# The last expert stage of a two-layer transformer kernel: one block, scaled rows delivered by adding writes

## The reference

```python
x = hidden_states                      # layernorm of the residual, 1024 x 256
confidences = sigmoid(x @ conf_w.T + conf_b)
bids = confidences * wealth            # 8 experts
top_bids, selected_experts = top_k(bids, 2)
routing_weights = softmax(top_bids)
combine = sum(one_hot(selected_experts) * routing_weights)
expert(x) = (silu(x @ gate.T) * (x @ up.T)) @ down.T      # inner size 1024
output = sum over experts of expert(x) * combine
out = residual + output
```

## Time and profile before

| What | Value |
|---|---|
| Time, median of 3 runs | 1272.21 us (1271.94 to 1273.88) |
| The profiled execution: its time, its span | 1274.95 us, 1273.2 us |
| PE busy over the span | 1144.7 us, 90% |
| DVE, ACT, POOL busy | 559.2 us (44%), 447.6 us (35%), 207.4 us (16%) |
| DMA | 169.43 MB, mean 133 GB/s |

### The profile page before, as it was taken

One profiled execution on the slowest core, in us unless ns is written; L12 is line 12 of the kernel. 1 busy time (PEld: TensorE's weight loads), 2 busy tenths in 40 slices (PEclk: granted clock), 3 DMA queues, 4 the chain that ended last, 5 costly groups with the idle time before them and its releaser, 6 DMA issues. The chain is left out here.

```text
span 1273.2 us, 19035 instructions
## 1 busy us (share of the span) xinstructions
PE 1144.7 (90%) x7144; PEld 726.4 (57%) x7168; DVE 559.2 (44%) x1586; ACT 447.6 (35%) x586; POOL 207.4 (16%) x336
## 2 busy tenths in 40 slices
PE   7989999999769999999577999999984599999993
PEld 4443333333558888888443333333244599999993
DVE  4757777771561111111365776666325212112222
ACT  4646666667321111111032455555642011111010
POOL 4652222224000000000113000000200111111110
PEclk8989999999869999999877999999995799999997
DMA  8656222002152444453149022210003799998843
GB/s 218 166 154 150 38 38 39 1 1 99 67 199 50 155 176 167 164 179 68 54 181 191 13 44 41 41 21 1 1 1 134 275 359 316 324 320 315 310 144 108
DMA packets 85956, 169.43 MB, mean 133 GB/s; under 512 B 7825, under 2 KB 58721, under 8 KB 83314
## 3 DMA queue, kind: packets, MB, share of 16 engines
q1 hardware_dynamic: 80050, 157.85, 39.8%
q0 software_dynamic: 2208, 6.03, 1.6%
q10 hardware_dynamic: 3616, 4.46, 1.2%
HBM read 148.34 MB, written 19.79 MB: 132 GB/s over the span
## 5 line engine op out<-in xcount | busy, mean ns | idle before, releaser
L1191 ACT ACTIVATE prob<-st_ps 128x1024 f32<-128x1024 f32 x256 | 253.9, 1022 | 188.7 <-PE st_ps L1089 105.5
L217 DVE CUSTOM_DVE_ANT_0 junk<-s_ps,bias_rows,mx 128x512 f32<-128x512 f32 x236 | 168.0, 748 | 64.1 <-PE s_ps L202 63.3
L1081 PE MATMUL st_ps<-q_stack,k_stack 100*128 100x512 bf16 x512 | 186.0, 387 | 10.4 <-ACTq L1170 3.5
L202 PE MATMUL s_ps<-k_stack,q_stack 97*128 97x512 bf16 x468 | 178.4, 391 | 11.0 <-DMA q_stack<-q_scr 6.3
L217 DVE CUSTOM_DVE_ANT_0 junk<-s_ps,bias_rows 128x512 f32<-128x512 f32 x232 | 153.3, 689 | 78.9 <-PE s_ps L202 78.3
L1577 PE MATMUL h_ps<-expert_in,w 128*128 (+1 forms) x704 | 155.0, 382 | 2.2 <-PEq L65 2.2
L1577 PEld LDWEIGHTS h_ps<-expert_in,w 128*128 128x128 f32 (+1 forms) x704 | 132.8, 189 | 22.9 <-issue 2.4
L1101 PE MATMUL o_ps<-prob,v_unit 128*32 128x512 f32 x1024 | 140.1, 601 | 1.0 <-ACT prob L1191 1.0
L202 PEld LDWEIGHTS s_ps<-k_stack,q_stack 97*128 97x128 bf16 x468 | 45.5, 99 | 146.0 <-DVE mx L217 82.4
L1980 ACT ACTIVATE silu<-gu_ps 128x512 f32<-128x512 f32 x46 | 27.5, 597 | 225.9 <-PE gu_ps L1936 225.9
L1607 ACT ACTIVATE gelu_out<-h_ps 128x256 f32<-128x256 f32 (+1 forms) x88 | 33.7, 383 | 182.2 <-PE h_ps L1577 182.2
(11 more groups left out here) (277 smaller groups left out, 1146.9 us busy)
## 6 DMA issues: line engine op xcount, KB each, us to landing
wg<-in_gateT SPq DMA_DIRECT2D x23, 1024.0 KB, 5.7
wu<-in_upT SPq DMA_DIRECT2D x23, 1024.0 KB, 9.2
wd<-in_downT SPq DMA_DIRECT2D x23, 1024.0 KB, 11.6
w<-in_w SPq DMA_DIRECT2D x16, 1368.0 KB
w<-in_w SPq DMA_DIRECT2D x8, 1280.0 KB
k_scr<-k_parts SPq DMA_DIRECT2D x48, 128.0 KB, 2.3
k_stack<-k_scr SPq DMA_DIRECT2D x16, 384.0 KB, 5.2
k_stack<-k_scr SPq DMA_DIRECT2D x16, 256.0 KB, 5.7
```

What stands on the lines that cost most here:

```text
L202: pe.matmul(self.ps[:, self.bank("job", u, j)], stack(self.pr.Q[b], MROW, i % 2, h, slice(qt * P, (qt + 1) * P)), stack(self.pr.K[b], MROW ...
L217: self.pr.nc.vector.tensor_tensor_reduce(out=self.junk[:, self.bank("job", u, j)], in0=self.ps[:, self.bank("job", u, j)], in1=self.m.bias ...
L1081: pe.matmul(st_ps[:, h], stack(K[b], ROWS, i % 2, h, slice(kt * P, (kt + 1) * P)), stack(Q[b], ROWS, i % 2, h, slice(0, SQ)), start=True, ...
L1191: nc.scalar.activation(prob[:, kt % 2, 2 * hp:2 * hp + 2], st_ps[:, 2 * hp:2 * hp + 2], ACT.Exp).then_inc(exp_done, 1)
```

## The change

The two blocks become one, with no barrier and no clearing of semaphores between router and tiles. In it:

- PE runs 14 transposes into the unused `xt_ps` before the norm's transposes and 20 after the 16 products (`stay_warm`).
- The rank comes from PE alone: `chosen` is bf16 with a ninth, empty group, and one product by the triangular matrix plus eight by ones accumulate all running sums (9 bf16 matmuls in place of 2 fp32 ones). The running sum over experts is a product with a comparison table `sooner` (made by POOL) and a reduction. The tile number comes from two scalings with rounding in place of 22 comparisons and a reduction.
- Of the 16 `hot_row` tables DVE makes 13 in one operation, POOL the last 3, one each; of the `hot_token` tables DVE makes the first column set, ACT the other two.
- `rows` is written before anything else that follows the products; `share`, `dest` and a new list `place` come after it.
- SP writes `pr.x` to the first 1024 rows of `row_scr`, and 128 more rows for the dump, right after the weights of tile 0. It then waits for `share`, writes it to DRAM (`shares`), and loads the weights of tile 1: gate at once, up and down only when `xg` of tiles 0 and 1 has landed.
- Per tile, POOL fetches one routing weight per row by a third indirect DMA (`fetch_share`), DVE multiplies the result by it as it copies it out of PSUM, and the delivery adds to `row_scr` (`compute_op=ALU.add`). Rows that stand for nothing go to the 128 dump rows.
- The output is two DRAM to DRAM transfers of 512 KB from `row_scr`; the reading back, the 16 DVE operations and the 8 writes are gone.

The removed side of the router stands in the code printed above. The core of the diff:

```diff
+        tps, lps, rps, ips = gu_ps[:, 0:2], gu_ps[:, 2], gu_ps[:, 3], y_ps[:, 0]
...
+        OWN = 13
...
+                load_gate(sp, 0, 0)
+                load_others(sp, 0, 0)
+                sp.dma_start(t["row_scr"][0:TOK].rearrange("(t p) d -> p t d", p=P), pr.x[:]).then_inc(x_saved, 16)
+                sp.dma_start(t["row_scr"][TOK:TOK + P], pr.x[:, 0]).then_inc(x_saved, 16)
+                sp.wait_ge(share_done, 1)
+                sp.dma_start(shares.rearrange("(t p k) -> p t k", p=P, k=2), share[:]).then_inc(share_out, 16)
+                sp.wait_ge(table_done, 1)
...
-                    load_weights(sp, e, T % NS)
+                    load_gate(sp, e, T % NS)
+                    if T == 1:
+                        for s in range(2):
+                            sp.wait_ge(xg_in[s], 16)
+                    load_others(sp, e, T % NS)
...
                 all_sent(sp)
-                for half in range(2):
...
-                for g in range(NT):
-                    sp.wait_ge(x_done, NT + g + 1)
-                    sp.dma_start(t["out"][g * P:(g + 1) * P], pr.x[:, g]).then_inc(x_out, 16)
...
+                for n in range(2):
+                    at = slice(n * TOK // 2, (n + 1) * TOK // 2)
+                    sp.dma_start(t["out"][at], t["row_scr"][at]).then_inc(x_out, 16)
...
+                g.tensor_scalar(sooner[:], below[:], 0.0, None, ALU.is_gt).then_inc(fill_done, 1)
+                pool.wait_ge(spot_done, 1)
+                pool.wait_ge(iota_done, 5)
+                for n in range(OWN - NT, NT):
+                    g.tensor_scalar(hot_row[:, NT + n], line[:], spot[:, 1, n:n + 1], None,
+                                    ALU.is_equal).then_inc(row_done, 1)
+                pool.wait_ge(rows_done, 1)
+                pool.wait_ge(y_out, 16)
...
+                def fetch_share(T):
+                    if T == 0:
+                        pool.wait_ge(dest_done, 1)
+                        pool.wait_ge(share_out, 16)
+                    if T >= 2:
+                        pool.wait_ge(y_copied, T - 1)
+                    pool.indirect_dma_start(out=row_share[:, T % 2], out_offset=None, in_=shares.unsqueeze(1),
+                                            in_offset=bass.IndirectOffsetOnAxis(ap=place[:, T:T + 1], axis=0),
+                                            bounds_check=2 * TOK - 1).then_inc(rs_in[T % 2], 16)
...
+                    if T == 0:
+                        pool.wait_ge(x_saved, 32)
...
-                    pool.indirect_dma_start(out=t["row_scr"],
+                    pool.indirect_dma_start(out=t["row_scr"][0:TOK + P],
                                             out_offset=bass.IndirectOffsetOnAxis(ap=dest[:, T:T + 1], axis=0),
-                                            in_=y_row[:, T % 2], in_offset=None,
-                                            bounds_check=3 * TOK - 1).then_inc(y_sent[T % 2], 16)
+                                            in_=y_row[:, T % 2], in_offset=None, bounds_check=TOK + P - 1,
+                                            compute_op=ALU.add).then_inc(y_sent[T % 2], 16)
...
+                fetch_share(0)
+                fetch_share(1)
...
+                    if T + 2 < TILES:
+                        fetch_share(T + 2)
...
+                def stay_warm(n):
+
+                    for _ in range(n):
+                        pe.transpose(xt_ps[:, 0, 0:P], pr.ident[:], pr.ident[:])
+
+                stay_warm(14)
...
+                pe.wait_ge(fill_done, 4)
+                pe.wait_ge(c_done, 1)
+                flat = chosen[:].rearrange("p g e -> p (g e)")
+                pe.matmul(rps[:, 0:(NT + 1) * E1], lower_bf[:], flat, start=True, stop=False)
+                for far in range(1, NT + 1):
+                    mm = pe.matmul(rps[:, far * E1:(NT + 1) * E1], ones_bf[:], flat[:, 0:(NT + 1 - far) * E1],
+                                   start=False, stop=(far == NT))
+                mm.then_inc(r_ready, 1)
+
+                pe.wait_ge(tok_done, 4)
+                for n in range(2 * NT):
+                    if n == 0:
+                        pe.wait_ge(own_row, 1)
+                    elif n >= OWN:
+                        pe.wait_ge(row_done, n - OWN + 1)
+                    mm = pe.matmul(ips[:, 0:3 * TILES], hot_row[:, n],
+                                   hot_token[:, n].rearrange("p o t -> p (o t)"),
+                                   start=(n == 0), stop=(n == 2 * NT - 1))
+                mm.then_inc(i_ready, 1)
+                stay_warm(20)
...
+                act.dma_start(t["y_scr"].rearrange("(t p) d -> p t d", p=P), pr.y[:]).then_inc(y_out, 16)
...
+                act.wait_ge(step_done, 1)
+                act.wait_ge(iota_done, 5)
+                nc.scalar.activation(hot_token[:, :, 1], hot_step[:], ACT.Copy, scale=low_t[:, 0:1]).then_inc(tok_done, 1)
+                for k in range(2):
+                    mine = slice(k * NT, (k + 1) * NT)
+                    nc.scalar.activation(hot_token[:, mine, 2], hot_step[:, mine], ACT.Copy,
+                                         scale=float(k + 1)).then_inc(tok_done, 1)
+                act.wait_ge(diff_done, 1)
+                nc.scalar.activation(low[:], low[:], ACT.Exp).then_inc(exp_done, 1)
...
+                v.tensor_tensor(chosen[:, 0:NT], one[:, 0], one[:, 1], ALU.add).then_inc(c_done, 1)
+                v.tensor_tensor(low[:], top[1][:], top[0][:], ALU.subtract).then_inc(diff_done, 1)
...
+                dve.wait_ge(r_ready, 1)
+                dve.wait_ge(iota_done, 5)
+                count = rps[:, NT * E1:(NT + 1) * E1]
+                link(v.tensor_tensor(fills[:], count.unsqueeze(2).broadcast_to([P, E1, TOK // P]),
+                                     part_line[:].unsqueeze(1).broadcast_to([P, E1, TOK // P]), ALU.is_gt))
+                link(v.tensor_reduce(parts[:], fills[:], AX.X, ALU.add))
+                link(v.tensor_scalar(parts[:], parts[:], 1.0, None, ALU.max))
+                link(v.tensor_tensor(below[:], sooner[:], parts[:].unsqueeze(1).broadcast_to([P, E1, E1]), ALU.mult))
+                link(v.tensor_reduce(start[:], below[:], AX.X, ALU.add))
+                link(v.scalar_tensor_tensor(out=rank[:], in0=by_e(start[:]), scalar=float(P),
+                                            in1=rps[:, 0:NT * E1].rearrange("p (g e) -> p g e", g=NT),
+                                            op0=ALU.mult, op1=ALU.add))
+                link(v.tensor_tensor(pick[:], one[:], rank[:].unsqueeze(1).broadcast_to([P, 2, NT, E1]), ALU.mult))
+                link(v.tensor_reduce(slot_f[:], pick[:], AX.X, ALU.add))
...
+                link(v.tensor_scalar(full[:], slot_f[:], 1.0 / P, 0.5 / P - 0.5, ALU.mult, ALU.add))
+                link(v.tensor_scalar(full[:], full[:], ROUND, ROUND, ALU.add, ALU.subtract))
+                v.scalar_tensor_tensor(out=spot[:], in0=full[:], scalar=-float(P), in1=slot_f[:],
+                                       op0=ALU.mult, op1=ALU.add).then_inc(spot_done, 1)
+                v.tensor_tensor(hot_step[:], full[:].rearrange("p k g -> p (k g)").unsqueeze(2)
+                                .broadcast_to([P, 2 * NT, TILES]),
+                                line[:, 0:TILES].unsqueeze(1).broadcast_to([P, 2 * NT, TILES]),
+                                ALU.is_equal).then_inc(step_done, 1)
+                dve.wait_ge(spot_done, 1)
+                v.tensor_tensor(hot_row[:, 0:OWN], spot[:].rearrange("p k g -> p (k g)")[:, 0:OWN].unsqueeze(2)
+                                .broadcast_to([P, OWN, P]), line[:].unsqueeze(1).broadcast_to([P, OWN, P]),
+                                ALU.is_equal).then_inc(own_row, 1)
+                dve.wait_ge(step_done, 1)
+                v.tensor_tensor(hot_token[:, :, 0].rearrange("p (k g) t -> p k g t", k=2),
+                                hot_step[:].rearrange("p (k g) t -> p k g t", k=2),
+                                high[:].unsqueeze(1).unsqueeze(3).broadcast_to([P, 2, NT, TILES]),
+                                ALU.mult).then_inc(tok_done, 1)
+                link(v.tensor_tensor(end[:], start[:], parts[:], ALU.add))
+                link(v.tensor_tensor(past[:], end[:, 0:7].unsqueeze(1).broadcast_to([P, TILES, 7]),
+                                     line[:, 0:TILES].unsqueeze(2).broadcast_to([P, TILES, 7]), ALU.is_le))
+                link(v.tensor_reduce(expert[:], past[:], AX.X, ALU.add))
+                v.tensor_copy(table[:], expert[:]).then_inc(table_done, 1)
+                dve.wait_ge(i_ready, 1)
+                rank_of = ips[:, 2 * TILES:3 * TILES]
+                link(v.tensor_copy(token_f[:, 0], ips[:, TILES:2 * TILES]))
+                v.scalar_tensor_tensor(out=rows[:], in0=ips[:, 0:TILES], scalar=float(P),
+                                       in1=token_f[:, 0], op0=ALU.mult, op1=ALU.add).then_inc(rows_done, 1)
+                dve.wait_ge(exp_done, 1)
+                link(v.tensor_scalar(top[0][:], low[:], 1.0, None, ALU.add))
```

(34 more changed lines are left out.)

286 lines of the change are left out of this document (87 added, 199 removed).

## The result

The changed kernel takes 1254.79 us in the median of 4 runs (1252.90 to 1255.87) against 1272.08 in the same comparison: a ratio of 0.9861, 95% interval 0.9845 to 0.9876. The forecast was 1250.9 with 1246 to 1259, so the measured time is 3.9 us above the forecast and inside the range. The profiled execution took 1254.66 us with a span of 1253.0; before, 1274.95 and 1273.2. So the profiles differ by 20.3 us, where the forecast had 21.3, and the medians by 17.3. Medians of the same kernel differ by up to 2.6 us from one comparison to the next (the kernel before: 1272.1 to 1274.7), so kernels of different comparisons are set beside each other by their ratios.

What follows compares the result with a forecast made beforehand. PE never waits between tiles, so only time ahead of tile 0 and behind tile 22 could be won. Gains of 21.3 us took the profiled 1274.95 to 1253.7, less 2.74 for the median: 1250.9 us, range 1246 to 1259.

Steps and rivals of the forecast that it cites:

- Norm and logits: Start of the last stage: 14 idle transposes raise PE's clock to 2.4 GHz; gain 3.4 us, bounds 0 and 4.6.
- Chain to the ranks: Router, from `chosen` to `fills`: nine bf16 products replace fp32 products, copy and running sums; gain 2.0 us.
- Tables and products: Router, from `spot_in` to the copy of the result: tables split over DVE, ACT and POOL; gain 0.9 us.
- Barrier: Between the copy of the result and the first indirect DMA: barrier gone, other work moved behind; gain 1.5 us.
- First gather: Ahead of tile 0: less weight traffic beside it, landing after 4.2 us instead of 6.47; gain 2.3 us.
- Clock of tile 0: Tile 0's first 64 matmuls: 20 idle transposes raise the clock, 9.11 us becomes 7.15; gain 1.9 us.
- Tile 1 and on: Tile 1's up and down weights wait for the second gather, about even; cost 0.3 us, bounds 0 and 3.
- End: Behind the last delivery's start: adding write, DRAM to DRAM copy and closing take 11.0 us instead of 19.5; gain 8.5.
- Rival 1: Norm and tile 0: the transposes don't hold the clock, both gains are lost; 1256.2 us, chance 0.13.
- Third transfer per tile: In each tile: POOL issues three indirect DMAs instead of two; cost 0 while an adding write lands within a tile.
- rival 4: Between tiles: adding writes set the pace once a landing exceeds 10.0 us; 1370 us, chance 0.04.
- Rival 2: At the end: adding write lands after 7.7 us and the copy takes 8.1; 1256.6 us, chance 0.12.

Runs made afterwards that it cites:

- e4: Changed kernel, but SP writes `share` and loads all three weights of tile 1 only once the first gather has landed: 1256.49 us, ratio 0.9868.
- e7: Changed kernel with `share` written to DRAM as 128 pieces of 64 bytes instead of 1024 of 8 bytes: 1254.79 us, ratio 0.9851.
- e11: e10, but SP loads all three weights of tile 1 without waiting for any gather: 1251.20 us, ratio 0.9815.
- e1: Changed kernel without both rows of idle transposes, the 14 and the 20: 1258.83 us, ratio 0.9882.
- e0: The changed kernel measured again, unaltered, as yardstick: 1254.48 us, ratio 0.9864.
- e8: e7, but SP loads up and down of tile 1 after the first gather alone, not the second: 1251.51 us, ratio 0.9828.
- e9: Changed kernel with the old end: plain deliveries, reading back, DVE, eight writes, no `share` or `pr.x` in DRAM: 1262.33 us, ratio 0.9916.
- e10: e8 with 30 idle transposes instead of 20 behind the 16 products: 1250.52 us, ratio 0.9810.
- e2: Changed kernel with 50 idle transposes instead of 20 behind the 16 products: 1254.76 us, ratio 0.9858.
- e6: Changed kernel with all 16 `hot_row` tables made on DVE, none on POOL: 1256.97 us, ratio 0.9874.

## Why the prediction was right, and where it was not

Term by term, in the two profiles, forecast and found (differences as in the section on the result):

| Term | Forecast | Found |
|---|---|---|
| Norm and logits | 3.4 | 4.25 |
| Chain to the ranks | 2.0 | 2.36 |
| Start of each expert | 0.5 | 0.49 |
| Tile number | 0.6 | 0.69 |
| Tables and products | 0.9 | 1.19 |
| Barrier | 1.5 | 1.38 |
| First gather | 2.3 | 0.85 |
| Clock of tile 0 | 1.9 | -0.41 |
| Tile 1 and on | -0.3 | -0.3 |
| End | 8.5 | 9.05 |
| Sum | 21.3 | 19.5 |

The stage began 0.65 us earlier in the profile after, which makes the 20.2 of the spans.

That the sum came out so near is partly luck: the gather and tile 0's clock fell short by 3.8 us together, the barrier by 0.1, and the other terms won 2.1 more than forecast.

- **Norm and logits**: right in mechanism, and the clock held for all of it, nearly the bound of 4.6. But not always: in e4, e7 and e11 `bids` came after 11.5 us, in the other eight profiles with the transposes after 9.5. The 14 are worth 2.3 or 4.3 by execution, and e1, without them, is at 13.8. The profiles show what went before. First the changed kernel, then e7, the 14 transposes and the first of the norm:

```profile
960.37 3.18 PE L1830 MATMUL xt_ps<-ident 128*128 128x128 f32 x14 [2.26 <-PEq L66]
963.74 1.30 PE L747 MATMUL gu_ps<-ident,y_tok 128*128 128x128 f32 x8 [0.19 <-DVE y_tok L731]
```

```profile
961.20 2.86 PE L1830 MATMUL xt_ps<-ident 128*128 128x128 f32 x14 [2.26 <-PEq L66]
964.58 1.30 PE L747 MATMUL gu_ps<-ident,y_tok 128*128 128x128 f32 x8 [0.52 <-DVE y_tok L731]
```

  The clock left over from attention fell later in the three: PEclk is 0.69 to 0.73 in the stage's first microsecond, 0.50 to 0.55 in the eight. So the 14 were done 0.3 us sooner and PE paused 0.5 us behind them instead of 0.2; the clock rose all the same and fell again some 7 us into the stage, with PE at work without a break. A few more transposes, to close that pause, are the obvious test; no run made it.
- **The DVE terms** were right within 0.4 us. Durations per column and per link carried over; where I was low, in the chain to the ranks, PE's nine products took 0.47 us instead of the 0.73 reckoned at 0.081 each, at the same granted clock of 0.50; they have 72 to 8 columns, the row's 69.
- **First gather**: the mechanism that I priced, less weight traffic beside it, is real, but the step "The write of `share` is 1024 pieces of 8 bytes, whose cost no row shows" was mis-sized. I put 0.5 us on it, and it was 1.9 to 2.4 (5.6 here and 6.1 in e0 against 3.7 in e7). Of the kernels with the new router, those that write it so right before the gather have gathers of 5.6 us or more; the others (e4, e7, e8, e9, e10, e11) are under 5.
- **Clock of tile 0**: wrong. The step that failed is "the gather lands 0.1 + 0.4 + 0.8 + 4.2 = 5.5 after that, so they do not delay it". I asked only whether the transposes would be too many. The last ones ran at 2.4 GHz, so the 20 took 3.7 us instead of 4.9, the gather came 1.4 us later, and the gap of 3.5 us lost what they had won: tile 0 took 9.4 us, not 7.15. Rival 1 was right for this half of the change and wrong for the other.
- **Tile 1's weights**: even, as forecast: the down weights landed at 1001.5, and tile 1's first gate matmul began at 1001.55. But that is luck. They were complete 12.8 us after the first gather and not 10, and PE wanted them just as much later, because tile 0 was slow. With tile 0 as fast as forecast PE waits, as e2 shows with 1.7 us: the two errors hid each other, and the slack of zero is why e2's gain turned into a wait.
- **Third transfer per tile, adding writes**: nothing between the tiles (241.7 us with them in e1, e6 and e11, as before), and landings rose only to 8.7 at most against 7.7, under the 10.0 at which rival 4 begins. One of my reasons against it was misread, though: not only the first third of the tiles has a full DMA load. In the profile before the DMA share is 0.85 to 1.05 in every stretch from 1010 to 1226.
- **The end**: forecast 11.0 from the last delivery's start, found 10.3; the add 0.4 and the copy 0.3 less than taken. The other figure for the copy, 4.4, was 1.3 too low by the same reckoning (6.6 us from its first issue to the end, less 0.9 for the closing). Rival 2 falls.
- **From the profile to the median**: the step "It ran 2.74 above the median of 1272.21, which I take off at the end" does not hold up. 31 more executions of the kernel before lie between 1270.7 and 1276.5 with medians of 1272.9 to 1274.7, so 1274.95 was no outlier, and a median of three may be off by as much as the step. Without it the forecast is 1253.7, against 1254.79; but that compares one execution's base with a median. The medians of the same comparison differ by 17.3 and 18.5 us (e0), the stages by 19.5 and 18.6. So of the 3.9 us by which the forecast was low, 1.8 are the stage's, and the rest no part of the stage accounts for.

What stays open: why the stages before it end up to 8 us apart in different profiles, e6's gather of 7.2 us, and whether more transposes ahead of the norm would hold the clock in every execution.

## What to carry to other kernels

Idle matmuls before a stage pay when they end where its work begins: measure the pause behind them, and remember that they run twice as fast once the clock is up. A wait that lets the clock fall costs more than its length: 2.5 us became 4.4 in e7, and 5.7 became 8.0 in e4. Before a small table goes to DRAM, count its pieces and not its bytes: an 8 KB write delayed a gather on the critical path by 2 us and, where it stood ahead of weights in their queue, held those up for about 4 (e4). And where a change frees time ahead of a prefetch with no slack, move the prefetch in the same change, or the gain becomes its wait.

## What the hardware showed that I had not expected

- A DRAM write of 1024 pieces of 8 bytes landed after 4.5 us; behind one, the transfer engines moved only 29 to 57 GB/s for 4 us (e4). As 128 pieces of 64 bytes it landed after 1.4.
- Two copies of 512 KB from DRAM to DRAM landed after 4.0 to 4.7 us each, less than reading back 2 MB (7.7 from its last issue).
- An indirect DMA that adds takes POOL 1.58 to 1.64 us to issue, 0.6 more than one that writes, and at the end of the kernel it landed after 3.5 to 3.9 us, where plain ones landed after 2.5 to 3.1.
- Solid work of transposes and 8-column matmuls did not raise the clock in 10 us, but once 14 transposes had raised it, the same work ran at 2.4 GHz to its end in eight of eleven profiles.
- Over a wait of 1.7 us the clock stayed up (e2); over waits of 2.5 (e7) and 5.7 us (e4) it fell, and so it did in e8 behind two pauses of 1.2 and 0.6 us.
